# Self-attention: moved probability blocks in runs of 2 KB, and a pair's last block transposition in its own double unit

## The reference, cut to what matters

```
DIM, HEADS, DHEAD = 160, 20, 64
h = layer_norm(x, g1, be1)
q = (h @ wq1), k = (h @ wk1), v = (h @ wv1)      # 512 x 1280 each, 20 heads of 64
scores = q @ k.T * 64 ** -0.5                    # per head, 512 x 512
attn = softmax(scores)
out = attn @ v                                   # per head, 512 x 64
x = out @ wo1 + bo1 + x
```

## Time and profile before

| | |
|---|---|
| median of 3 runs | 1036.35 us (1035.43 to 1042.49) |
| the profiled execution | 1033.81 us, span 1032.0 us |
| mean granted TensorE clock | 0.973 |
| TensorE busy | 918.9 us, 89% |
| VectorE busy | 699.6 us, 68% |
| ScalarE busy | 558.6 us, 54% |
| GpSimd busy | 380.6 us, 37% |
| DMA packets | 117530, of which 116261 are under 2 KB |

### The profile page before, as it was taken

One profiled execution on the slowest core, in us unless ns is written; L12 is line 12 of the kernel. 1 busy time (PEld: TensorE's weight loads), 2 busy tenths in 40 slices (PEclk: granted clock), 3 DMA queues, 4 the chain that ended last, 5 costly groups with the idle time before them and its releaser, 6 DMA issues.

```text
span 1032.0 us, 16880 instructions
## 1 busy us (share of the span) xinstructions
PE 918.9 (89%) x5736; PEld 645.1 (63%) x5736; DVE 699.6 (68%) x1211; ACT 558.6 (54%) x1292; POOL 380.6 (37%) x493
## 2 busy tenths in 40 slices
PE   7999977888989988989988889988869999999998
PEld 4566665445556654556655547645427689999887
DVE  3766647676777576767577766676724889999563
ACT  2666634655666455666456655556633555455442
POOL 2676623343434234334234334333320034344220
PEclk9999989999999999999999999999989999999999
DMA  6400050333233223333223332223330340000000
GB/s 140 88 1 1 1 148 9 75 82 83 65 79 72 48 65 83 77 71 71 48 64 83 82 82 68 48 64 71 80 82 14 102 103 1 1 1 1 2 26 26
DMA packets 117530, 59.59 MB, mean 58 GB/s; under 512 B 18805, under 2 KB 116261, under 8 KB 117445
## 3 DMA queue, kind: packets, MB, share of 16 engines
q1 hardware_dynamic: 117445, 58.50, 24.2%
HBM read 11.26 MB, written 1.31 MB: 12 GB/s over the span
## 4 chain that ended last, share of the span: by engine, by line
PE 55%; DVE 13%; issue 9%; ACT 3%; SPq 2%; POOL 1%; DMA 1%; DVEq 0%; ACTq 0%; POOLq 0%
PE banks L435 13%; PE banks L409 9%; PE banks L421 5%; PE banks L453 4%; DVE sa_negmax L602 3%; PE banks L224 3%; PE banks L227 2%; PE banks L225 2%; PE banks L226 2%; PE banks L1696 2%; PE banks L1988 2%; SPq L369 2%; PE banks L232 2%; DVE ca_top L1831 2%; DVE ca_probs L1836 1%
## 5 line engine op out<-in xcount | busy, mean ns | idle before, releaser
L695 POOL TENSOR_SCALAR sa_probs_even<-sa_probs_even,sa_inverse 128x512 f32<-128x512 f32 x160 | 111.3, 696 | 365.0 <-DVE sa_inverse L606 364.9
L435 PE MATMUL banks<-sa_turned_even,sa_v 128*64 128x512 f32 x320 | 167.6, 650 | 61.4 <-issue 50.1
L602 DVE TENSOR_REDUCE sa_negmax<-banks 128x2 f32<-128x1024 f32 x160 | 187.9, 1215 | 12.3 <-PE banks L409 12.0
L538 ACT ACTIVATE sa_probs_even<-banks,sa_negmax 128x512 f32<-128x512 f32 x160 | 109.9, 687 | 123.0 <-DVE sa_negmax L602 123.0
L435 PE MATMUL banks<-sa_turned_odd,sa_v 128*64 128x512 f32 x320 | 168.6, 653 | 0.0
L614 DVE STREAM_TRANSPOSE sa_in_blocks<-sa_probs_even 128x512 f32<-128x512 f32 x160 | 112.7, 705 | 40.3 <-POOL sa_probs_even L695 39.9
L409 PE MATMUL banks<-sa_k_parts,sa_q_parts 64*128 64x512 f32 x960 | 135.0, 410 | 5.2 <-ACT sa_probs_odd L538 5.2
L435 PEld LDWEIGHTS banks<-sa_turned_even,sa_v 128*64 128x64 f32 x320 | 39.1, 142 | 137.8 <-issue 126.4
L695 POOL TENSOR_SCALAR sa_probs_odd<-sa_probs_odd,sa_inverse 128x512 f32<-128x512 f32 x160 | 111.1, 695 | 0.0
L538 ACT ACTIVATE sa_probs_odd<-banks,sa_negmax 128x512 f32<-128x512 f32 x160 | 109.6, 685 | 0.0
L409 PEld LDWEIGHTS banks<-sa_k_parts,sa_q_parts 64*128 64x128 f32 x960 | 83.7, 184 | 36.2 <-issue 15.0
(11 more groups left out here) (223 smaller groups left out, 1925.0 us busy)
## 6 DMA issues: line engine op xcount, KB each, us to landing
sa_turned_even<-sa_in_blocks SPq DMA_DIRECT2D x640, 64.0 KB, 2.1
w_o<-in_L_xattn_wo SPq DMA_DIRECT2D x2, 800.0 KB, 9.1
out<-x SPq DMA_DIRECT2D x4, 320.0 KB, 2.4
w_q_t<-in_L_xattn_wq_t SPq DMA_DIRECT2D x1, 1120.0 KB, 10.6
fold_values<-ca_turned SPq DMA_DIRECT2D x5, 192.5 KB
x<-in_x SPq DMA_DIRECT2D x1, 960.0 KB, 5.2
fold_values<-ca_probs SPq DMA_DIRECT2D x4, 192.5 KB
w_q_t<-in_L_xattn_wq SPq DMA_DIRECT2D x1, 640.0 KB, 6.0
```

The lines of the kernel that those rows point to most:

```text
L435: last = pe.matmul(b_out[e * HD:(e + 1) * HD, :], v[:, v_buf(b, j), k, c:c + HD], turned, start=(k == 0), stop=(k == QT - 1))
L538: act.activation(to, b_scores[u % 2][:, e, :], ACT.Exp, bias=negmax[:, u % RING, e:e + 1], accum_out=total[:, u % RING, e:e + 1]).then_inc ...
L602: dve.tensor_reduce(negmax[:, u % RING, :], b_scores[u % 2], AX_X, ALU.max, negate=True).then_inc(s_max.sem, 1)
L695: pool.tensor_scalar(p, p, inverse[:, u % RING, e:e + 1], 1.0, ALU.mult, ALU.mult).then_inc(s_norm.sem, 1)
```

## The change

Two things change. First the layout: `in_blocks` is ordered by target group, then key tile, query tile and token, and `turned_even` by source group, then key tile. What one DMA moves is then one contiguous run of 512 float32 values (2 KB) in each of 32 partitions, on both sides; before it was four runs of 128 values (512 bytes). The number of DMAs and their bytes stay. The transposition writes and PV reads with other strides to match. Second the order on VectorE: each double unit transposes units `m` and `m + 1`, the second one at its end, in place of `m - 1` and `m`; the prologue transposes one unit more.

```diff
-        in_blocks = sb("in_blocks", [P, 2, S // SQ, P])
-        turned_even = sb("turned_even", [P, 2, QT, S])
+        in_blocks = sb("in_blocks", [P, 2, NS, S])
+        turned_even = sb("turned_even", [P, 2, NS, S])
...
-            source = in_blocks[:].rearrange("p a (k j) c -> p a k j c", j=NS)
-            target = turned_even[:].rearrange("p a k (i c) -> p a k i c", i=NS)
...
-                            sp.dma_start(target[rows(k), j % 2, :, i, :], source[rows(i), j % 2, :, k, :]).then_inc(moved(b, j)[0], 16)
+                            sp.dma_start(turned_even[rows(k), j % 2, i, :], in_blocks[rows(i), j % 2, k, :]).then_inc(moved(b, j)[0], 16)
...
-                by_token = lambda ap: ap.rearrange("p (i q c) -> p q i c", i=NS, q=QT)
-                for e, turned in enumerate((by_token(turned_even[:, j % 2, k, :]), turned_odd[:, k, :])):
+                by_token = turned_even[:, j % 2, :, k * P:(k + 1) * P].rearrange("p i (q c) -> p q i c", q=QT)
+                for e, turned in enumerate((by_token, turned_odd[:, k, :])):
...
-                dve.transpose(in_blocks[:, j % 2, :, q * SQ:(q + 1) * SQ],
-                              probs_even[:, q, :].rearrange("p (j c) -> p j c", c=SQ)).then_inc(s_blocks.sem, 1)
+                to = in_blocks[:, j % 2, :, :].rearrange("p j (k q c) -> p k j q c", k=QT, q=QT)[:, :, :, q, :]
+                dve.transpose(to, probs_even[:, q, :].rearrange("p (k j c) -> p k j c", j=NS, c=SQ)).then_inc(s_blocks.sem, 1)
...
             turn_blocks(0, 2)
+            turn_blocks(0, 3)
...
                     over(maxima, b, m + 1, NU, more)
-                    over(turn_blocks, b, m - 1, NU, more)
...
                         over(rest_q, b, d // 2 + 3, NPAIR, more)
+                    over(turn_blocks, b, m + 1, NU, more)
```

## The result

The median went from 1036.21 us (of four runs; the 1036.35 above is of three) to 988.69 us (987.51 to 989.92), a ratio of 0.9525 with a 95% interval of 0.9491 to 0.956. The forecast was 990 us, in a range of 970 to 1012. The profiled execution took 987.51 us with a span of 985.7, against 1033.81 and 1032.0.

The account below looks back on a forecast made before the run. The prediction took the move chain, with TensorE's wait on top, as the bound (14.9 us an interval). VectorE's 12.4 us round would replace it: 42.9 us less between PVs and 2 at the start, -45 to 989, stated as 990, range 970 to 1012.

Parts of the forecast that it names:

- PV waits for the moves, and the order removes the wait: Even PV, line 435: TensorE's 61.4 us idle is for the last moved block; moves starting some 2.9 us earlier leave no stall.
- VectorE's round goes from 11.05 to 12.35 us: VectorE, two double units: waiting for GpSimd's scale at the transposition's new place adds 0.90 and 0.40 us.
- That round sets the time: VectorE's 12.4 us exceeds TensorE's 11.8 and becomes the bound in 33 intervals, 409.2 us.
- Runs of 2 KB take an issue from 0.60 to 0.42 us: SP's queue: sixteen moves take 7.4 us, landing 8.9 us after the transposition in place of 11.7.
- The shape of the transfer from DRAM: Transfers with one long run in each of 32 partitions, 0.417 us an issue, taken as the new moves' nearest row.
- rival (1): Moves stay at 0.60 us an issue and stall each pair, 0.5 us net in 33 intervals, 16 us: 1006 us; 15%.
- the prediction's own list of what would show it wrong: Moves issuing at 0.60 us, the transposition over 0.75 us, or VectorE's rounds nearer 11.8 or 13.5 us.
- The Trainium skill's rule: DMA moves: line rate from runs of 512 B, so longer runs bring nothing and latency stays 11.7 us; priced under rival (1).
- The sum: First to last PV: 109.0 output projection, 409.2 other intervals, 20 normalization, 3.0 last pair; 541.2 us, 42.9 less; 2 at the start.
- rival 4: VectorE's transposition, output pieces 2 KB apart: a doubled time would add 112 us, less 45, about 1100 us; 4%.

Follow-up runs that it names:

- the copies: The changed kernel plus one more VectorE copy of the 128 x 128 identity at each double unit's end, 80 in all: 1001.03 us, ratio 0.9664.
- late exponentials: The changed kernel with four of a pair's sixteen moves issued by ScalarE, two ahead of its exponentials: 998.85 us, ratio 0.9649.
- faster moves alone: The changed kernel with three of a pair's moves issued by ScalarE at the even double unit's end, thirteen by SP: 989.63 us, ratio 0.9554.
- a longer TensorE: The changed kernel with one 128 x 128 TensorE transposition made twice in each unit, 160 more in all: 995.28 us, ratio 0.9612.
- a shorter VectorE round alone: The changed kernel with only a pair's last transposition early, the other back behind the maxima: 988.71 us, ratio 0.9541.

## Why the prediction was right

- **PV waits for the moves, and the order removes the wait.** Right: idle time 61.4 to 16.3 us (I expected below 10), and the order alone does it (19.6 us, 990.18 us).
- **VectorE's round goes from 11.05 to 12.35 us.** Right to the hundredth where it runs undisturbed. Its waits before the transpositions were to rise to 68 us and rose to 65.0.
- **That round sets the time.** Right in the 33 intervals without an output projection. What lengthens VectorE's chain shows nearly in full (0.27 us a round by the copies, 0.43 us a pair by late exponentials), whereas faster moves alone, or a longer TensorE, leave the round at 12.35 us. What the prediction didn't see is how near the next limit is: a shorter VectorE round alone changes nothing, since the moves then hold TensorE, and through it VectorE.
- **Runs of 2 KB take an issue from 0.60 to 0.42 us.** Wrong: 0.591. The shape of the transfer from DRAM was the wrong neighbour; between SBUF and SBUF the time stayed with the kind of transfer. The moves land 11.5 us or more after the transposition, not 8.9 (10.0 to 10.4 us of issues and the same 1.5 us, an estimate). This was rival (1), but its price, 16 us, wasn't paid: with the old issue time the order alone is at 990.18. I had put TensorE's waits on top of VectorE's round; most run beside it. An issue near 0.60 was on the prediction's own list of what would show it wrong. With this value in the sum it would have said 1006 us: two errors, an issue time too short and a price too high for a late move, made up for each other, and in that the 990 was luck. It was no luck that VectorE's round was the bound and how long it is.
- **The Trainium skill's rule** ("DMA: Bandwidth & Descriptors", Specifications: line rate from runs of 512 B) named the right outcome for the layout, 0.9973 by itself, though what the runs show is SP's time for one issue, not the engines' rate.
- **The sum.** 541.2 us from first to last PV against 538.5 measured, and 2 us for the start against 0.8. The output projection's six intervals were set at 109.0 as TensorE's own: longer TensorE work lengthens them (23.06 to 24.00 us for the two double units) and longer VectorE work doesn't (23.06). VectorE's work for the next normalization was set at 5 us a batch, and its double units 6, 7 and 14 are together 3.9 us longer than their neighbours (7.53, 7.30 and 7.51 us, against 6.12 and 6.23).
- **The scattered output (rival 4)** costs nothing that shows: the transposition took 704 ns in the kernel with the layout alone, 705 before, and 710 in both kernels with the new order, the one with the old layout among them.

## What to carry to other kernels

When a transfer is late, look first at when it starts and how many issues stand in its queue; longer runs didn't shorten an issue between SBUF and SBUF. Price an earlier start by laying out the engine's instructions one behind another, with what each waits for at its new place: here that gave the new round to 0.01 us. Once several paths end within half a microsecond, relieve them together and expect each alone to give nothing; and look at what a remedy costs the engine that takes the work over.

## What the runs showed of the hardware

An SBUF-to-SBUF DMA takes SP 0.591 us to issue with 32 runs of 2 KB and 0.601 with 128 runs of 512 bytes, where transfers of 32 long rows from DRAM take 0.417. Two issues on ScalarE's queue took 1.41 us and pushed its next exponentials back although the engine itself was idle. A copy recorded at 0.18 us lengthened VectorE's chain by 0.13 to 0.14. The longest issue of these moves on SP was 1.8 to 2.1 us in every kernel, where the median is 0.59 or 0.60; why is open.
